# Query tiles from the last to the first inside each head of a differential-attention layer

## Chip, cores and metric

The kernel runs on 1 core of one Trainium2 chip. The metric is the device time of one execution in microseconds (us), the median of the runs shown.

## What is computed

One layer: differential attention with a causal mask, layer norm, a gated feed-forward network, layer norm. The part that the change touches is the attention core. With 2 batches of 2,048 tokens, 16 heads, head size 16 and values of size 32:

```python
s1 = jnp.einsum('bhqd,bhkd->bhqk', q1, k1) * scale
s2 = jnp.einsum('bhqd,bhkd->bhqk', q2, k2) * scale
a1 = jax.nn.softmax(jnp.where(causal, s1, neg_inf), axis=-1)
a2 = jax.nn.softmax(jnp.where(causal, s2, neg_inf), axis=-1)
comb = a1 - lam[None, :, None, None] * a2
out = jnp.einsum('bhqk,bhkv->bhqv', comb, v)
```

After it `out` is normalized per head, projected, added to `x` and normalized; then the feed-forward part follows.

## The kernel before

Five phases run one after the other, each with its own buffers: projections, a phase for the softmax shift, the attention (`attention_phase`), and the rest of the layer (`finish_phase`), which has a first form with rounded weights (the one that runs here) and a second one that is skipped. Only `attention_phase` is changed.

**Tiles and steps.** Inside a head the 2,048 queries are four query tiles t = 0, 1, 2, 3 of 512, and the keys are 16 blocks j of 128. A step (t, j) handles one key block against one query tile, for both batches and both softmaxes. Causality leaves tile t with 4t + 4 steps, 40 in a head. In the last four key blocks of a tile (the diagonal ones) the queries ahead of the key block are dropped, so a step is 512, 384, 256 or 128 queries wide; the four diagonal steps of a tile are a "512" with a mask, a "384", a "256" and a "128". The list `STEPS` writes the order out by hand. Named by width, with F for 512, it is:

- tile 0: F, 256, 128, 384
- tile 1: F, 256, F, 384, F, F, F, 128
- tile 2: F, F, 256, F, F, F, 384, F, F, F, F, 128
- tile 3: F, F, F, F, 256, F, F, F, F, 384, F, F, F, F, F, 128

**Units.** ScalarE does the exponentials. A step is two units, one per batch, except that a 256 or a 128 takes both batches in one. So a head has 72 units. Three score slots (`s_ps`, `SLOTS` = 3) hold one unit each, and four buffers (`probs`) one step each.

**TensorE's order.** For each step k TensorE issues the scores of k (L827), then the weighing with the values of step k - 3 (`LAG`, L847), and two steps after the weighing that ends a tile the transposes of its sums (`turn`, `TURN_LAG`, L855). So a tile's transposes stand behind the fifth step of what follows the tile:

```python
use(h, u, first, k - LAG)
if k - TURN_LAG in END:
    turn(h, END.index(k - TURN_LAG))
```

The scores of a unit wait until ScalarE has emptied its slot, three units earlier; the exponential (L808) waits for its scores; GpSimd masks the diagonal corner (L792); the weighing waits for exponential and mask.

**The sums.** Tile t adds up in PSUM bank t % 2. VectorE copies the finished bank out (L892), TensorE transposes it back into the bank, VectorE copies that out (L894), which frees the bank for the tile after the next, and six small operations (L902 to L913) finish the tile in `diff`. After the fourth tile of a head SyncE stores `diff` (L772) and then, once the head's weighing is over, loads the stacks of the head after the next (L517, L533, L540). Heads follow without a barrier: the scores of the next head are issued while the last three steps of this one are still to be weighed.

Of the kernel before, what the change touches and what calls it, by code (L numbers as in the profile page):

```python
# [29 lines left out]
QUERY_TILES = SEQ // TILE  # L30
# [658 lines left out]
def attention_phase(nc, keep, heads, qk_parts, shift, values, diffs):  # L689
# [2 lines left out]

    STEPS = [(0, j) for j in (0, 2, 3, 1)]
    for t in range(1, QUERY_TILES):
        third = SUBS * t // 3
        order = list(range(SUBS * t)) + [SUBS * t, SUBS * t + 3]
        order.insert(2 * third + SUBS * t % 3 // 2, SUBS * t + 1)
        order.insert(third, SUBS * t + 2)  # L700
        STEPS += [(t, j) for j in order]
    END = [max(k for k, (t, _) in enumerate(STEPS) if t == tile) for tile in range(QUERY_TILES)]

    UNITS = []
    for k, (t, j) in enumerate(STEPS):
        UNITS += [(k, [0, 1])] if j - SUBS * t >= SUBS // 2 else [(k, [0]), (k, [1])]
    NU = len(UNITS)
    LAST_UNIT = [max(n for n, (step, _) in enumerate(UNITS) if step == k) for k in range(len(STEPS))]
    LAG = 3
    TURN_LAG = 2  # L710

    MASKS = [sum(j >= SUBS * t for t, j in STEPS[:k + 1]) for k in range(len(STEPS))]
    NS = len(STEPS)
    NT = QUERY_TILES
    SLOTS = 3
    PROBS = 4
# [4 lines left out]
    def window(t, j):  # L721

        return max(0, j - SUBS * t) * PARTS

    with Room(nc, "attn") as room:
# [18 lines left out]
        probs_free = room.sem("probs_free")  # L744
        sums_copied = room.sem("sums_copied")
        turned = room.sem("turned")
        sums_bank_free = room.sem("sums_bank_free")
# [8 lines left out]
        def all_heads(head):  # L756

            for h in range(HEADS):
                head(h, h % 2, h // 2, h == 0, h == LAST)

        @block.sync
        def _(sp):
            def head(h, u, r, first, last):
                if not last:

                    sp.wait_ge(probs_free, PROBS + NS * h)
                    load_head(sp.dma_start, heads, qk_parts, values, h + 1, 1 - u)
                    load_shift(sp.dma_start, heads, shift, h + 1, 1 - u)

                sp.wait_ge(diff_ready, NT * h + NT)  # L770
                for b in range(BATCH):
                    sp.dma_start(diffs[b * KEY_BLOCKS:(b + 1) * KEY_BLOCKS, :, h, :].rearrange("k p n -> p k n"),  # L772
                                 diff[:, :, :].rearrange("p (k b) n -> p k b n", b=BATCH)[:, :, b, :]).then_inc(stored, 16)


            load_shift(sp.dma_start, heads, shift, 0, 0)
            all_heads(head)
            sp.wait_ge(stored, STORES + STORES * HEADS)
# [31 lines left out]
        @block.tensor  # L810
        def _(pe):
            def scores(h, u, r, first, n):

                k, batches = UNITS[n]
                t, j = STEPS[k]
                off = window(t, j)
                width = TILE - off
                if n == 0:

                    pe.wait_ge(loaded[u], 16 * HEAD_LOADS * r + 16 * HEAD_LOADS)  # L820
                if not first or n >= SLOTS:

                    pe.wait_ge(exp_done, NU * h + n - SLOTS + 1)
                for place, b in enumerate(batches):
                    for s in range(2):
                        rows = slice(s * HALF_ROWS, s * HALF_ROWS + STACK_ROWS)
                        last = nc.tensor.matmul(s_ps[n % SLOTS][:, s, place * width:(place + 1) * width],  # L827
                                                k_sb[u][rows, b * SEQ + j * PARTS:b * SEQ + (j + 1) * PARTS],
                                                q_sb[u][rows, b * SEQ + t * TILE + off:b * SEQ + (t + 1) * TILE], start=True, stop=True)
                last.then_inc(scored, 1)  # L830

            def weigh(h, u, k):

                t, j = STEPS[k]
                off = window(t, j)
                sums = sums_ps[t % 2]
                pe.wait_ge(exp_done, NU * h + LAST_UNIT[k] + 1)
                if j >= SUBS * t:

                    pe.wait_ge(masked, SUBS * NT * h + MASKS[k])  # L840
                if j == 0:

                    pe.wait_ge(sums_bank_free, NT * h + t + 1)
                for b in range(BATCH):
                    for s in range(2):
                        c = 2 * b + s
                        last = nc.tensor.matmul(sums[c * D:(c + 1) * D, off:TILE], v_sb[u][:, b * KEY_BLOCKS + j, :], probs[k % PROBS][:, b, s, off:TILE],  # L847
                                                start=(j == 0), stop=(k == END[t]))
                last.then_inc(probs_free, 1)

            def turn(h, t):

                pe.wait_ge(sums_copied, NT * h + t + 1)
                for i in range(SUBS):
                    last = nc.tensor.transpose(sums_ps[t % 2][:, i * PARTS:(i + 1) * PARTS], sums_sb[:, i * PARTS:(i + 1) * PARTS], keep["ident"][:, :])  # L855
                last.then_inc(turned, 1)

            def use(h, u, first, k):

                if k < 0:  # L860
                    if first:
                        return
                    h, u, k = h - 1, 1 - u, k + NS
                weigh(h, u, k)
                if k - TURN_LAG in END:
                    turn(h, END.index(k - TURN_LAG))
                elif k - TURN_LAG + NS in END and not first:
                    turn(h - 1, END.index(k - TURN_LAG + NS))

            def head(h, u, r, first, last):  # L870
                for k in range(NS):
                    for n, (step, _) in enumerate(UNITS):
                        if step == k:
                            scores(h, u, r, first, n)
                    use(h, u, first, k - LAG)
                if last:
                    for k in range(NS - LAG, NS):
                        use(h, u, first, k)
                    turn(h, QUERY_TILES - 1)

            all_heads(head)

        @block.vector
        def _(dve):
            def tile(h, t):
                n = NT * h + t
                bank = sums_ps[t % 2]


                dve.wait_ge(probs_free, PROBS + NS * h + END[t] + 1)  # L890
                dve.wait_ge(turned, n + 1)
                nc.vector.tensor_copy(sums_sb[:, :], bank[:, :]).then_inc(sums_copied, 1)  # L892
                dve.wait_ge(turned, n + 2)
                nc.vector.tensor_copy(raw[:, :, :, :].rearrange("p k s d -> p (k s d)"), bank[:, :]).then_inc(sums_bank_free, 1)  # L894


                v0 = VEC * n
                rows = diff[:, SUBS * BATCH * t:SUBS * BATCH * (t + 1), :]
                wide = [PARTS, SUBS * BATCH, D - 1]

                dve.wait_ge(sums_bank_free, 2 + n + 1)
                nc.vector.reciprocal(recip[:, :, :], raw[:, :, :, D - 1]).then_inc(vec, 1)  # L902
                dve.wait_ge(vec, v0 + 1)
                nc.vector.tensor_tensor(first[:, :, :], raw[:, :, 0, 0:D - 1], recip[:, :, 0:1].to_broadcast(wide), ALU.mult).then_inc(vec, 1)
                nc.vector.tensor_tensor(second[:, :, :], raw[:, :, 1, 0:D - 1], recip[:, :, 1:2].to_broadcast(wide), ALU.mult).then_inc(vec, 1)
                dve.wait_ge(vec, v0 + 3)

                dve.wait_ge(stored, STORES * h + STORES)
                nc.vector.scalar_tensor_tensor(rows[:, :, 0:D - 1], second[:, :, :], keep["neg_lam"][:, bass.ts(h, 1)], first[:, :, :], ALU.mult, ALU.add).then_inc(vec, 1)
                dve.wait_ge(vec, v0 + 4)  # L910
                nc.vector.tensor_reduce(total[:, :], rows[:, :, 0:D - 1], AXIS.X, ALU.add).then_inc(vec, 1)
                dve.wait_ge(vec, v0 + 5)
                nc.vector.tensor_scalar(rows[:, :, D - 1], total[:, :], -1.0, None, ALU.mult).then_inc(vec, 1)  # L913
                dve.wait_ge(vec, v0 + 6)
                dve.sem_inc(diff_ready, 1)

            for h in range(HEADS):
                for t in range(QUERY_TILES):
                    tile(h, t)


def turn_weights_phase(nc, keep, ffn_w, whole_w):
# [613 lines left out]
```

## Time and profile before

| | |
|---|---|
| median of 3 runs | 2055.02 us (2047.17 to 2059.04) |
| the profiled execution, its own time | 2058.76 us |
| its span, first to last instruction | 2057.0 us |
| attention phase, first scores to the issue of the last stores | 232.04 to 1279.42 us |
| one head in the middle of it | 64.61 us |
| TensorE (matmul) busy | 1917.9 us (93%) |
| ScalarE busy | 1468.7 us (71%) |
| VectorE busy | 724.0 us (35%) |

A row of a timeline gives the start in us, how long the piece lasts, engine, line, operation, the tiles, and how many instructions were joined in it; in brackets stands how long the engine had been idle before it and what released it. Pieces that follow one another with hardly a gap are joined. PE is TensorE, ACT ScalarE, DVE VectorE, SPq the queue of SyncE. The end of a matmul is modelled and overlaps the start of the next, so the cost of a piece on TensorE is the distance from its start to the next start.

### The profile page before, as it was taken

How to read it: one execution, taken by the hardware profiler on the slowest of the kernel's cores; microseconds unless marked ns; L12 is line 12 of the kernel's file. 1: busy time of each engine (PE TensorE's matmuls, PEld its weight loads, DVE VectorE, ACT ScalarE, POOL GpSimd, SP SyncE). 2: the span in 40 equal slices, each digit the busy share in tenths (PEclk: the TensorE clock that was granted, in tenths of full speed). 3: DMA queues.
4: the chain of work that ended last, by engine and by line, in shares of the span. 5: the costliest groups of instructions: out<-in, count | busy, mean ns of one | idle time of the engine just before them, and what ended most of it. 6: DMA issues, size and time to landing. Idle time of an engine off the chain costs nothing. (4 is left out here: it accounts for less than half of the span.)

```text
span 2057.0 us, 32689 instructions
## 1 busy us (share of the span) xinstructions
PE 1917.9 (93%) x12400; PEld 1091.7 (53%) x12400; DVE 724.0 (35%) x1543; ACT 1468.7 (71%) x1876; POOL 200.3 (10%) x300
## 2 busy tenths in 40 slices
PE   7995499999999999999999997599999999999996
PEld 6883133333333333333333332488888788888885
DVE  5776012222122221222112221445463545445342
ACT  5663499999999999999999997244454445445452
POOL 0001011111111111111111110000000000000000
PEclk9997699999999999999999999699999999999998
DMA  8997906643466434653356510200000000000000
GB/s 265 364 348 216 140 2 84 84 58 53 59 84 84 54 54 62 84 73 54 47 78 84 72 24 11 72 22 11 32 11 31 22 31 31 12 31 11 11 11 12
DMA packets 137048, 148.55 MB, mean 72 GB/s; under 512 B 76000, under 2 KB 108256, under 8 KB 133760
## 3 DMA queue, kind: packets, MB, share of 16 engines
q1 hardware_dynamic: 134768, 140.55, 34.2%
q10 hardware_dynamic: 1888, 5.24, 1.3%
q8 instruction: 104, 1.70, 0.4%
q0 software_dynamic: 240, 0.66, 0.2%
q14 instruction: 48, 0.39, 0.1%
HBM read 90.85 MB, written 55.57 MB: 71 GB/s over the span
## 5 line engine op out<-in xcount | busy, mean ns | idle before, releaser
L808 ACT ACTIVATE attn_probs<-attn_s_ps 128x1024 f32<-128x1024 f32 (+2 forms) x1152 | 1014.0, 1042 | 75.3 <-PE attn_s_ps L827 71.5
L847 PE MATMUL attn_sums_ps<-attn_probs,heads_v 128*32 128x512 f32 (+3 forms) x5120 | 603.1, 543 | 0.6 <-issue 0.6
L827 PE MATMUL attn_s_ps<-heads_q,heads_k 50*128 50x512 f32 (+3 forms) x2560 | 472.5, 431 | 67.2 <-DMA heads_q<-shift 49.5
L827 PEld LDWEIGHTS attn_s_ps<-heads_q,heads_k 50*128 50x128 f32 x2560 | 216.6, 185 | 543.1 <-ACT attn_probs L808 457.9
L1331 ACT ACTIVATE split_whole<-split_hid_ps,hs 128x512 f32<-128x512 f32 x128 | 88.3, 690 | 274.4 <-PE split_hid_ps L1245 274.2
L892 DVE COPY attn_sums_sb<-attn_sums_ps 128x512 f32<-128x512 f32 x64 | 44.3, 692 | 639.1 <-PE attn_sums_ps L847 635.7
L792 POOL TENSOR_SCALAR_AFFINE_SELECT attn_probs<-attn_probs 128x512 f32<-128x512 f32 x256 | 160.4, 635 | 919.8 <-ACT attn_probs L808 917.9
L1245 PE MATMUL split_hid_ps<-split_hid_b,h2t_r 128*128 128x512 f32 x1024 | 240.6, 392 | 0.0
L1245 PE MATMUL split_hid_ps<-split_hid_a,h1t_r 128*128 128x512 f32 x1024 | 238.0, 391 | 0.0
L1245 PEld LDWEIGHTS split_hid_ps<-split_hid_a,h1t_r 128*128 128x128 f32 x1024 | 190.0, 188 | 41.1 <-DVE split_hid_a L1473 1.3
L1245 PEld LDWEIGHTS split_hid_ps<-split_hid_b,h2t_r 128*128 128x128 f32 x1024 | 189.8, 188 | 38.0
L847 PEld LDWEIGHTS attn_sums_ps<-attn_probs,heads_v 128*32 128x32 f32 x5120 | 101.4, 108 | 165.3 <-issue 122.8
L1316 ACT ACTIVATE split_gate<-split_hid_ps,s 128x512 f32<-128x512 f32 x64 | 44.1, 689 | 94.4 <-PE split_hid_ps L1229 94.4
L894 DVE COPY attn_raw<-attn_sums_ps 128x512 f32<-128x512 f32 x64 | 44.2, 691 | 183.3 <-PE attn_sums_ps L855 183.3
L1479 DVE TENSOR_TENSOR split_hid_a<-split_whole,split_hid_a 128x512 fp32r<-128x512 f32 x64 | 44.3, 692 | 179.4 <-ACT split_hid_a L1334 179.4
L468 PE MATMUL proj_qk_ps<-proj_xt,proj_wqk_high 128*128 128x512 f32 x256 | 95.8, 420 | 1.5 <-DVE proj_xt L383 1.5
L1155 POOL TENSOR_TENSOR split_square<-split_heads 128x512 f32<-128x512 f32 x28 | 28.6, 1041 | 591.3 <-DVE split_head_var L1358 338.6
L1479 DVE TENSOR_TENSOR split_hid_b<-split_whole,split_hid_b 128x512 fp32r<-128x512 f32 x64 | 44.1, 689 | 94.8 <-ACT split_hid_b L1334 94.7
L1229 PE MATMUL split_hid_ps<-split_xt,w1t_r 128*128 128x512 f32 x256 | 72.2, 405 | 4.6 <-issue 3.2
L1229 PE MATMUL split_hid_ps<-split_xt,w2t_r 128*128 128x512 f32 x256 | 70.2, 397 | 0.0
L1469 DVE SCALAR_TENSOR_TENSOR split_whole<-split_hid_ps,s,split_gate 128x512 f32<-128x512 f32 x64 | 48.0, 751 | 54.3 <-ACT split_gate L1316 54.3
L1262 PE MATMUL split_y_ps<-w3t_r,split_hid_a 128*128 128x256 f32 x512 | 64.7, 284 | 2.6 <-DVE split_y L1503 2.6
(123 smaller groups left out, 1571.2 us busy)
## 6 DMA issues: line engine op xcount, KB each, us to landing
qk_parts<-proj_parts SPq DMA_DIRECT2D x64, 512.0 KB, 5.7
heads_q<-qk_parts SPq DMA_DIRECT2D x90, 256.0 KB
heads_k<-qk_parts SPq DMA_DIRECT2D x90, 256.0 KB
proj_w_rows<-in_L_ffn_h_w SPq DMA_DIRECT2D x16, 512.0 KB, 6.8
values<-proj_v SPq DMA_DIRECT2D x8, 1024.0 KB, 6.0
diffs<-attn_diff SPq DMA_DIRECT2D x32, 256.0 KB, 4.5
split_heads<-diffs SPq DMA_DIRECT2D x8, 1024.0 KB, 5.7
heads_v<-values SPq DMA_DIRECT2D x15, 512.0 KB
```

The source lines that it names most:

```text
L468: last = nc.tensor.matmul(qk_ps[m % 4][:, :], wqk[a][:, kind, c, o * PARTS:(o + 1) * PARTS], xt[u][b][:, c, :], start=(c == 0 and n == 0), ...
L792: pool.affine_select(out=corner, in_=corner, compare_op=ALU.is_ge, fill=0.0, base=0, pattern=[[0, 2 * BATCH], [1, PARTS]], channel_multipl ...
L808: nc.scalar.activation(weights, side_by_side, ACT.Exp, scale=SCALE).then_inc(exp_done, 1)
L827: last = nc.tensor.matmul(s_ps[n % SLOTS][:, s, place * width:(place + 1) * width], k_sb[u][rows, b * SEQ + j * PARTS:b * SEQ + (j + 1) * ...
L847: last = nc.tensor.matmul(sums[c * D:(c + 1) * D, off:TILE], v_sb[u][:, b * KEY_BLOCKS + j, :], probs[k % PROBS][:, b, s, off:TILE], start ...
L892: nc.vector.tensor_copy(sums_sb[:, :], bank[:, :]).then_inc(sums_copied, 1)
L1229: last = nc.tensor.matmul(bank[:, :], weights[w][:, c, m * PARTS:(m + 1) * PARTS], xt[k][:, c, :], start=(c == 0 and k == 0), stop=(c == E ...
L1245: last = nc.tensor.matmul(hid_ps[m % 4][:, :], weights[w][:, c, m * PARTS:(m + 1) * PARTS], hid[k][:, c, :], start=(c == 0 and k == 0), st ...
L1262: last = nc.tensor.matmul(y_ps[s % 2][:, s // 2, :], hid_a[k][:, c, s * PARTS:(s + 1) * PARTS], weights["w3t"][:, c, :], start=(c == 0 and ...
L1331: nc.scalar.activation(gelu, hid_ps[m % 4][:, :], ACT.Gelu, scale=keep[s][:, m:m + 1]).then_inc(gelu_done, 1)
L1469: nc.vector.scalar_tensor_tensor(product, hid_ps[2 * (m % 2) + 1][:, :], keep["s2"][:, m:m + 1], gate[m % 2][:, :], ALU.mult, ALU.mult).th ...
L1479: nc.vector.tensor_tensor(hid[1][:, m, :], whole[m % 2][:, :], hid[0][:, m, :].bitcast(F32), ALU.subtract).then_inc(hid_low, 1)
```

## The change

`STEPS` is built with the tiles in the order 3, 2, 1, 0. Inside a tile the order of the key blocks stays. The counters that ran with the tile's number now run with its place in the order.

```diff
-    STEPS = [(0, j) for j in (0, 2, 3, 1)]
-    for t in range(1, QUERY_TILES):
+    TILE_ORDER = list(reversed(range(QUERY_TILES)))
+    STEPS = []
+    for t in TILE_ORDER[:-1]:
...
         STEPS += [(t, j) for j in order]
-    END = [max(k for k, (t, _) in enumerate(STEPS) if t == tile) for tile in range(QUERY_TILES)]
+    STEPS += [(0, j) for j in (0, 2, 3, 1)]
+    END = [max(k for k, (t, _) in enumerate(STEPS) if t == tile) for tile in TILE_ORDER]
...
-                    pe.wait_ge(sums_bank_free, NT * h + t + 1)
+                    pe.wait_ge(sums_bank_free, NT * h + TILE_ORDER.index(t) + 1)
...
-                                                start=(j == 0), stop=(k == END[t]))
+                                                start=(j == 0), stop=(k in END))
...
-            def turn(h, t):
-
-                pe.wait_ge(sums_copied, NT * h + t + 1)
+            def turn(h, place):
+
+                t = TILE_ORDER[place]
+                pe.wait_ge(sums_copied, NT * h + place + 1)
...
-            def tile(h, t):
-                n = NT * h + t
+            def tile(h, place):
+                n = NT * h + place
+                t = TILE_ORDER[place]
...
-                dve.wait_ge(probs_free, PROBS + NS * h + END[t] + 1)
+                dve.wait_ge(probs_free, PROBS + NS * h + END[place] + 1)
...
-                for t in range(QUERY_TILES):
-                    tile(h, t)
+                for place in range(QUERY_TILES):
+                    tile(h, place)
```

What moves is shown at two places of TensorE's stream. `attn_s_ps` are the three score slots, `attn_sums_ps` the two banks of sums, `attn_sums_sb` is VectorE's copy of a finished bank; two score rows of 512 (or 384) columns are the two units of one step.

**First place, TensorE, where tile 1 begins.** Before, tile 1 follows tile 0 (its first three steps, a head other than the first):

```order
L827 MATMUL attn_s_ps0<-heads_q1,heads_k1 128x512 x2
L827 MATMUL attn_s_ps1<-heads_q1,heads_k1 128x512 x2
L847 MATMUL attn_sums_ps0<-attn_probs1,heads_v1 32x256 x4
L855 MATMUL attn_sums_ps1<-ident,attn_sums_sb 128x128 x4
L827 MATMUL attn_s_ps2<-heads_q1,heads_k1 128x256 x4
L847 MATMUL attn_sums_ps0<-attn_probs2,heads_v1 32x128 x4
L827 MATMUL attn_s_ps0<-heads_q1,heads_k1 128x512 x2
L827 MATMUL attn_s_ps1<-heads_q1,heads_k1 128x512 x2
L847 MATMUL attn_sums_ps0<-attn_probs3,heads_v1 32x384 x4
```

With the change it follows tile 2:

```order
L829 MATMUL attn_s_ps1<-heads_q0,heads_k0 128x512 x2
L829 MATMUL attn_s_ps2<-heads_q0,heads_k0 128x512 x2
L849 MATMUL attn_sums_ps0<-attn_probs1,heads_v0 32x512 x4
L829 MATMUL attn_s_ps0<-heads_q0,heads_k0 128x256 x4
L849 MATMUL attn_sums_ps0<-attn_probs2,heads_v0 32x512 x4
L829 MATMUL attn_s_ps1<-heads_q0,heads_k0 128x512 x2
L829 MATMUL attn_s_ps2<-heads_q0,heads_k0 128x512 x2
L849 MATMUL attn_sums_ps0<-attn_probs3,heads_v0 32x128 x4
```

The scores are the same (F, 256, F). Behind them stood the weighing of tile 0's narrow steps and the transposes of tile 3; now there stand two full steps and the 128 of tile 2.

**Second place, TensorE, the end of the phase.** Before, the last three weighings are tile 3's, and only its own transposes come after them:

```order
L827 MATMUL attn_s_ps2<-heads_q1,heads_k1 128x128 x4
L847 MATMUL attn_sums_ps1<-attn_probs0,heads_v1 32x512 x4
L847 MATMUL attn_sums_ps1<-attn_probs1,heads_v1 32x512 x4
L847 MATMUL attn_sums_ps1<-attn_probs2,heads_v1 32x512 x4
L847 MATMUL attn_sums_ps1<-attn_probs3,heads_v1 32x128 x4
L855 MATMUL attn_sums_ps1<-ident,attn_sums_sb 128x128 x4
```

With the change:

```order
L829 MATMUL attn_s_ps1<-heads_q1,heads_k1 128x384 x2
L829 MATMUL attn_s_ps2<-heads_q1,heads_k1 128x384 x2
L849 MATMUL attn_sums_ps0<-attn_probs0,heads_v1 32x512 x4
L849 MATMUL attn_sums_ps0<-attn_probs1,heads_v1 32x256 x4
L858 MATMUL attn_sums_ps1<-ident,attn_sums_sb 128x128 x4
L849 MATMUL attn_sums_ps0<-attn_probs2,heads_v1 32x128 x4
L849 MATMUL attn_sums_ps0<-attn_probs3,heads_v1 32x384 x4
L858 MATMUL attn_sums_ps0<-ident,attn_sums_sb 128x128 x4
```

The last tile is now tile 0, four narrow steps long, and the transposes of tile 1 stand between its weighings, two steps ahead of its own.

## Rows read from the trace of the kernel before

**Rows 1.** The page, part 5: the exponentials (busy, mean ns | idle before, releaser).

```profile
L808 ACT ACTIVATE attn_probs<-attn_s_ps 128x1024 f32<-128x1024 f32 (+2 forms) x1152 | 1014.0, 1042 | 75.3 <-PE attn_s_ps L827 71.5
```

**Rows 2.** Timeline of ScalarE, 560 to 640 us, one period of a head.

```profile
559.21 2.85 ACT L808 ACTIVATE attn_probs<-attn_s_ps 128x1024 f32<-128x1024 f32 x3 [0.21 <-PE attn_s_ps L827]
562.23 33.90 ACT L808 ACTIVATE attn_probs<-attn_s_ps 128x512 f32<-128x512 f32 x39 [0.16 <-PE attn_s_ps L827]
596.32 8.36 ACT L808 ACTIVATE attn_probs<-attn_s_ps 128x1024 f32<-128x1024 f32 x9 [0.20 <-PE attn_s_ps L827]
605.11 18.50 ACT L808 ACTIVATE attn_probs<-attn_s_ps 128x1024 f32<-128x1024 f32 x21 [0.43 <-PE attn_s_ps L827]
623.83 2.85 ACT L808 ACTIVATE attn_probs<-attn_s_ps 128x1024 f32<-128x1024 f32 x3 [0.21 <-PE attn_s_ps L827]
```

**Rows 3.** Groups by form, ScalarE, 304 to 1240 us: the full unit.

```profile
L808 ACT ACTIVATE attn_probs<-attn_s_ps 128x1024 f32<-128x1024 f32 x865 | 808.7, 1088 | 15.9 <-PE attn_s_ps L827 14.2
```

**Rows 4.** Timeline of TensorE, 558.5 to 566.5 us: from tile 3 into tile 0.

```profile
558.60 0.73 PE L827 MATMUL attn_s_ps<-heads_q,heads_k 50*128 50x512 f32 x4
...
560.26 0.50 PE L827 MATMUL attn_s_ps<-heads_q,heads_k 50*128 50x256 f32 x4
560.69 1.07 PE L847 MATMUL attn_sums_ps<-attn_probs,heads_v 128*32 128x512 f32 x8
561.69 0.44 PE L827 MATMUL attn_s_ps<-heads_q,heads_k 50*128 50x128 f32 x4
562.06 0.43 PE L847 MATMUL attn_sums_ps<-attn_probs,heads_v 128*32 128x128 f32 x8
562.41 0.64 PE L827 MATMUL attn_s_ps<-heads_q,heads_k 50*128 50x384 f32 x4
562.98 1.07 PE L847 MATMUL attn_sums_ps<-attn_probs,heads_v 128*32 128x512 f32 x8
563.98 0.73 PE L827 MATMUL attn_s_ps<-heads_q,heads_k 50*128 50x512 f32 x4
564.63 0.64 PE L847 MATMUL attn_sums_ps<-attn_probs,heads_v 128*32 128x256 f32 x8
565.21 0.66 PE L855 MATMUL attn_sums_ps<-ident,attn_sums_sb 128*128 128x128 f32 x4
565.79 0.50 PE L827 MATMUL attn_s_ps<-heads_q,heads_k 50*128 50x256 f32 x4
```

**Rows 5.** Timeline of ScalarE, 512.0 to 512.9 us: from tile 1 into tile 2.

```profile
511.31 1.77 ACT L808 ACTIVATE attn_probs<-attn_s_ps 128x512 f32<-128x512 f32 x2
```

**Rows 6.** Timeline of TensorE, 497 to 566 us.

```profile
502.63 0.85 PE L847 MATMUL attn_sums_ps<-attn_probs,heads_v 128*32 128x384 f32 x8
...
511.45 0.74 PE L827 MATMUL attn_s_ps<-heads_q,heads_k 50*128 50x512 f32 x4
...
536.45 0.50 PE L827 MATMUL attn_s_ps<-heads_q,heads_k 50*128 50x512 f32 x2 [0.41 <-ACT attn_probs L808]
...
539.89 0.73 PE L827 MATMUL attn_s_ps<-heads_q,heads_k 50*128 50x512 f32 x4
```

**Rows 7.** Timeline of VectorE, 497 to 566 us: tile 3, then tile 0.

```profile
501.29 0.69 DVE L894 COPY attn_raw<-attn_sums_ps 128x512 f32<-128x512 f32 x1 [2.66 <-PE attn_sums_ps L855]
...
504.76 0.69 DVE L892 COPY attn_sums_sb<-attn_sums_ps 128x512 f32<-128x512 f32 x1 [0.23 <-DVE attn_diff L913]
```

**Rows 8.** Timeline of all engines, 1240 to 1300 us: the end of the phase.

```profile
1271.42 0.44 PE L827 MATMUL attn_s_ps<-heads_q,heads_k 50*128 50x128 f32 x4
...
1274.98 0.69 DVE L892 COPY attn_sums_sb<-attn_sums_ps 128x512 f32<-128x512 f32 x1 [17.87 <-PE attn_sums_ps L847]
...
1279.42 1.44 SPq L772 DMA_DIRECT2D diffs<-attn_diff  x2
```

**Rows 9.** Windows: busy us of PE, PEld, DVE, ACT, POOL, then PEclk, DMA share, GB/s.

```profile
232.00:246.70 14.70, 13.87 (x72) 5.22 (x72) 0.69 (x1) 11.16 (x13) 3.13 (x5) 0.52 1.03 125
536.00:558.60 22.60, 21.77 (x160) 6.82 (x158) 3.02 (x8) 22.17 (x26) 1.27 (x2) 1.00 0.00 1
```

## The prediction

> **What bounds the kernel now.** Only the attention phase changes, so I read it alone. The page's groups come first: the exponentials on ScalarE are busy 1014.0 us of a phase of some 1047, and 71.5 of the 75.3 us that ScalarE idled ahead of them were ended by scores [rows 1]. So inside the phase ScalarE is the bound, and what the order can change is the time it waits for scores. The timeline of ScalarE shows where that is: a head repeats after 623.83 - 559.21 = 64.62 us, with four visible gaps [rows 2].
>
> To price the gaps I need the cost of one unit. Nine full units last 8.36 us [rows 2], one alone 1.09 [rows 3], so the next starts every (8.36 - 1.09) / 8 = 0.91 us. A 384 unit (768 elements of 1024) is then about 0.68, a 128 unit (512) 0.45. A head has 60 full-sized units, 8 of 384 and 4 of 128: 54.5 + 5.4 + 1.8 = 61.6 us. **ScalarE loses 3.0 us in each head**, and these 3.0 us are the whole subject.
>
> Where they go, each as the next start less the start before plus its work [rows 2]:
> - tile 3 into tile 0, first F after the 128: 21 units from 605.11 are 18.1 us of work, free at 623.2, next at 623.83: 0.60.
> - the 128 of tile 0: free at 559.21 + 2.72 = 561.93, starts at 562.23: 0.30.
> - the two next steps of tile 0. TensorE's rows give the time from the start of a score piece to the start of its exponential: 0.61 for an F (558.60 to 559.21), 0.54 for a 128 (561.69 to 562.23) [rows 2, 4]. The 384 at 562.41 and the F at 563.98 so start 0.28 and 0.26 late.
> - tile 1 into tile 2: the 128 starts at 511.31, is free at 511.76, the F issued at 511.45 starts at 512.06: 0.30 [rows 5, 6].
> - tile 2 into tile 3: 0.64 ahead of 605.11 [rows 2], behind the transposes of tile 2; and about 0.5 ahead of 596.32, from what is left of 39 units. The rest, 0.15, lies at the transposes inside tile 2.
>
> Each loss is a place where TensorE, which does a full step in 0.66 + 1.00 = 1.66 us against ScalarE's 1.81, has had extra work or a narrow unit has shortened the backlog. In long runs of F it catches up and waits for a slot (0.41 at 536.45 [rows 6]); then the backlog is three units again.
>
> **The change, part by part.** Nothing is added or removed: the same 40 steps, 72 units, 4 transposes and 4 VectorE chains per head. Only the junctions between tiles differ: 3|0, 0|1, 1|2, 2|3 become 3|2, 2|1, 1|0, 0|3. TensorE's prices, start to start [rows 4]: scores F 0.66, 384 0.57, 256 0.43, 128 0.36; weighing F 1.00, 256 0.58, 128 0.35; transposes 0.58. The weighing of a 384 is 0.85 less the modelled 0.07, 0.78 [rows 6].
>
> - **3|2**: the tail of tile 3 costs what it did, 0.60; the head of tile 2 behind a gap is as it was, 0.15. Sum 0.75 (before these were 0.60 and 0.15 too, elsewhere).
> - **2|1**: the tail of tile 2 costs 0.5. Then F, 256, F is issued behind full weighings instead of tile 0's narrow ones. From the start of tile 1: the second F is issued at 1.66 + 0.43 + 1.00 = 3.09 and can start at 3.70; ScalarE started at 0.61 and is free after three units at 3.34. New loss 0.36. Behind it stands the weighing of only 128 (0.35), and TensorE pulls ahead. At the transposes of tile 2, behind the fifth step, I walk on the same way: the next F can start at 8.5, ScalarE is free at 8.7, no loss. Sum 0.86.
> - **1|0**: going on with the walk, tile 0's first F can start at 12.9 and ScalarE is free at 12.7: 0.2 in place of 0.60. Then the 128, the 384 as before: 0.30 + 0.28. Sum 0.78.
> - **0|3**: the F after the 384 0.26 as before. The transposes of tile 1 stand behind it as those of tile 3 did. Then come weighings of 128 and 384, TensorE runs ahead until it waits for a slot, as it did at 536.45, and from there to the F behind the transposes (539.89 [rows 6]) the instructions are word for word those of before: 0.64. Sum 0.90.
>
> After: 0.75 + 0.86 + 0.78 + 0.90 = 3.29 against 3.0: **+0.27 us per head**, over 16 heads +4.3. As the errors of such a walk are about 0.1 at each of four junctions, its bounds are -0.1 and +0.6 per head: -2 to +10.
>
> **The end of the phase.** Before, the last unit (the 128 of tile 3) was issued at 1271.42, the last copy began at 1274.98, the stores went out at 1279.42 [rows 8]; its exponential starts 0.92 after the issue and is 0.45 of work, so 6.6 us pass from ScalarE's last work to the stores. After, the last scores are tile 0's 384. Behind them come weighing F, weighing 256 and the transposes of tile 1 at 0.57 + 1.00 + 0.58 = 2.15. VectorE copies the result 0.70 later (the transposes at 565.21 [rows 4] stood a period earlier at 500.59, the copy at 501.29 [rows 7]) and needs 504.76 - 501.29 = 3.47 us for the chain of that tile before it takes the next copy [rows 7]; TensorE's own last weighing would have been over sooner. The last copy so starts at 6.3, the stores 4.44 later at 10.7. ScalarE's work ended at 1.9. 8.8 against 6.6: **+2.2 us**. Inside the phase the same queue on VectorE costs nothing, because tile 0's transposes are four steps later.
>
> **The start.** In head 0 the granted clock is 0.52 of full for 14.7 us while TensorE is busy 13.87 of them [rows 9], the lower level of 1.2 GHz. There TensorE is the bound in either order, and 13.87 us at half speed are the same work. Tile 3 first puts more exponentials per matmul into this stretch, tile 0 first fewer; I take 0, bounds -2 and +2.
>
> **What costs nothing.** The bank wait: tile 3's first weighing waits for the bank of tile 1, freed by a copy behind the transposes, four steps earlier, as now between 3 and 1. The stores and the loads of the head after the next leave SyncE later by about 1.3 us (tile 0's transposes are behind the fifth step of a wide tile, not a narrow one), and the loads are over long ahead of the next head: DMA share 0.00 in the last 22.6 us [rows 9]. Without that cover each us late would be a us for the head.
>
> **Sum**: +4.3 + 2.2 + 0 = +6.5 us. On the profiled execution's own 2058.76 that is 2065.3. The median of the runs is 3.74 lower, so the forecast as a median is **2061.5 us**, its own range 2053 to 2069 (bounds of the walk, of the start, and some 4 us between runs).
>
> **Rivals.**
> - **Slower, the transposes starve tile 1.** At tile 1's fifth step my walk leaves 0.2 us of backlog. If it is under 0, the transposes cost ScalarE there what they cost in tile 3, up to 0.64. For it: tile 1 has the fewest F in a row ahead of them. Against: the weighing of 128 just before. Decides once TensorE is 0.2 us later than I have it. +10 over 16 heads: 2072.
> - **Faster, tile 0 behind a backlog.** If tile 1's run of F leaves a full backlog, the losses of tile 0 (0.2 + 0.30 + 0.28 + 0.26) and tile 1's 0.36 vanish: -22, so 2040. Against: at 1|2 the same tail left 0.30 of loss [rows 5].
> - **No change.** The junction losses only move, and the end costs its 2.2: 2057. The narrow tile stands between two others in both orders.
> - **The clock.** TensorE is idle for 0.8 us of the 14.7 and the clock stays at its lower level. If wide steps make it rise a third of the way in, some 10 us run at 2.4 instead of 1.2 GHz: -5, so 2056.5. The Trainium skill, page "TensorE: Matmul & The Clock Gate", Part 1, says that the throttled clock is the default and that sustained activity releases it; by that rule the denser start should be released sooner, and the time would be this rival's. The trace of before speaks against it, with 13.87 busy us at the lower level [rows 9], so it gets little.
>
> **How the numbers follow.** Forecast 0.65, no change 0.13, the clock 0.05, slower 0.12, faster 0.05. A measurement of this kernel can tell about 0.5%, 10.3 us, from no change. Faster by more: the faster rival, 0.05. Slower by more: the slower rival and the upper edge of the forecast, 0.17. Same: 0.78. The range takes the no-change case and the lower half of the slower one: 2050 to 2071.
>
> **What would show it.** In the profile after, a head should repeat after 64.9 us. ScalarE should show gaps at the start of tile 2, of tile 1 and again 2.7 us later, a smaller one at tile 0's start, and one of 0.43 behind the transposes in tile 3. At the end the last L892 copy should be released by L913, not by a weighing. I am wrong if the period is under 64.5 or over 65.3, if ScalarE has a gap behind tile 1's fifth step, or if TensorE ever waits for L892 or L894 inside the phase.

## The result, and the profile after

| | before | after |
|---|---|---|
| median of 20 runs | 2055.09 us | 2059.76 us |
| lowest to highest | 2047.17 to 2059.04 | 2055.38 to 2065.88 |
| ratio, 95% interval | | 1.0027, 1.0017 to 1.0037 |
| profiled execution, span | 2057.0 us | 2055.6 us |
| first scores to the issue of the last stores | 1047.4 us | 1049.3 us |
| one head in the middle | 64.62 us | 64.95 us |

The change makes the kernel 4.7 us (0.2%) slower, clear of noise, and less than the 0.5% that the prediction counted as no change. The two profiled executions stand the other way round, 2058.76 us before and 2057.33 after (spans 2057.0 and 2055.6). By the traces the attention phase itself is 1.9 us longer after the change; the phases ahead of it took 2.1 us less (it begins at 229.93 in place of 232.04) and the rest of the layer 1.2 us less, though neither was changed. What else parts the two is told below.

The page after (busy us, share and count of TensorE; then the groups that answer to [rows 1] and the copies of finished banks):

```profile
PE 1917.7 (93%) x12400; PEld 1089.8 (53%) x12400; DVE 719.2 (35%) x1543; ACT 1470.8 (72%) x1876; POOL 200.9 (10%) x300
...
L810 ACT ACTIVATE attn_probs<-attn_s_ps 128x1024 f32<-128x1024 f32 (+2 forms) x1152 | 1015.8, 1033 | 71.7 <-PE attn_s_ps L829 67.9
...
L896 DVE COPY attn_sums_sb<-attn_sums_ps 128x512 f32<-128x512 f32 x64 | 44.3, 692 | 654.7 <-PE attn_sums_ps L849 651.1
```

Idle time ahead of the exponentials did not grow in this page, 71.7 us for 75.3 before, since the wait ahead of the phase (47.3 us, before 49.1), the first head and two stalled heads of the kernel before are in it. In every other head it rose, from 1.3 to 1.4 or 1.5 us. The page cannot show that; the timeline can. ScalarE from 560 to 700 us, one period of a head, answering to [rows 2] (start, length, joined instructions, idle time ahead):

```profile
565.49 18.51 ACT L810 ACTIVATE attn_probs<-attn_s_ps 128x1024 f32<-128x1024 f32 x21 [0.43 <-PE attn_s_ps L829]
584.20 19.45 ACT L810 ACTIVATE attn_probs<-attn_s_ps 128x1024 f32<-128x1024 f32 x22 [0.21 <-PE attn_s_ps L829]
603.85 2.86 ACT L810 ACTIVATE attn_probs<-attn_s_ps 128x1024 f32<-128x1024 f32 x3 [0.20 <-PE attn_s_ps L829]
606.93 12.22 ACT L810 ACTIVATE attn_probs<-attn_s_ps 128x1024 f32<-128x1024 f32 x14 [0.23 <-PE attn_s_ps L829]
619.33 10.68 ACT L810 ACTIVATE attn_probs<-attn_s_ps 128x512 f32<-128x512 f32 x12 [0.18 <-PE attn_s_ps L829]
630.43 18.50 ACT L810 ACTIVATE attn_probs<-attn_s_ps 128x1024 f32<-128x1024 f32 x21 [0.43 <-PE attn_s_ps L829]
```

Two of these rows are joined across a tile's end. From 565.49 to 630.43 a head repeats after 64.94 us, and there are five visible gaps where [rows 2] has four. The new one is 0.23 ahead of 606.93, three units behind the start of tile 1 (603.85). With the unit costs of the prediction the losses are: 0.6 at 584.20 (tile 3 into 2), 0.6 from there to 603.85 (inside tile 2, and 2 into 1), 0.37 at 606.93, 0.6 up to 619.33 (tile 1 into 0 and the 128), 1.1 up to 630.43 (the rest of tile 0, 0 into 3, the transposes): 3.3 us. A loss is larger than the idle time in brackets, because the records of neighbouring exponentials overlap; where a row runs on, a loss can hide in it.

TensorE at the same place, the start of tile 1, with the F behind the 256, the slot wait and the transposes:

```profile
603.25 0.73 PE L829 MATMUL attn_s_ps<-heads_q,heads_k 50*128 50x512 f32 x4
...
606.33 0.73 PE L829 MATMUL attn_s_ps<-heads_q,heads_k 50*128 50x512 f32 x4
...
608.01 0.44 PE L829 MATMUL attn_s_ps<-heads_q,heads_k 50*128 50x384 f32 x2 [0.22 <-ACT attn_probs L810]
...
610.63 0.66 PE L858 MATMUL attn_sums_ps<-ident,attn_sums_sb 128*128 128x128 f32 x4
```

The F behind the 256 is issued 606.33 - 603.25 = 3.08 us behind the start of the tile. One and a half steps later TensorE already waits 0.22 us for a slot, so at the transposes (610.63) ScalarE has a backlog and shows no gap.

The end of the phase (TensorE's last scores, the transposes of tile 1, the last copy, the stores), answering to [rows 8]:

```profile
1268.79 2.24 ACT L810 ACTIVATE attn_probs<-attn_s_ps 128x512 f32<-128x512 f32 x3 [0.18 <-PE attn_s_ps L829]
...
1268.97 0.61 PE L829 MATMUL attn_s_ps<-heads_q,heads_k 50*128 50x384 f32 x4
...
1270.94 0.66 PE L858 MATMUL attn_sums_ps<-ident,attn_sums_sb 128*128 128x128 f32 x4
...
1271.64 0.69 DVE L898 COPY attn_raw<-attn_sums_ps 128x512 f32<-128x512 f32 x1 [1.83 <-PE attn_sums_ps L858]
...
1274.79 0.69 DVE L896 COPY attn_sums_sb<-attn_sums_ps 128x512 f32<-128x512 f32 x1 [0.23 <-DVE attn_diff L917]
...
1275.54 0.66 PE L858 MATMUL attn_sums_ps<-ident,attn_sums_sb 128*128 128x128 f32 x4 [2.71 <-DVE attn_sums_sb L896]
...
1279.24 1.45 SPq L774 DMA_DIRECT2D diffs<-attn_diff  x2
```

The last copy is released by L917, the end of tile 1's chain on VectorE, and TensorE stands 2.71 us until it is there (0.81 before). From the last scores to the stores it takes 10.27 us, before 8.00. ScalarE's last work ends at 1271.03, so 8.2 us pass from there to the stores; before they were 6.2 (ScalarE's last row ended at 1273.18, the stores went out at 1279.42): +2.0 us. Counted as the prediction counts it, from the start of the last exponential plus its cost, it is 8.3 against 6.6, +1.7 us.

### The profile page after: what moved, and what is told of

Read it like the earlier page. It is cut to its first block and busy times, and to the rows that moved or that the text cites. A ratio compares the mean times of both kernels' runs of the same rounds, so it can differ in the third digit from the quotient of the medians.

```text
span 2055.6 us, 32689 instructions
## 1 busy us (share of the span) xinstructions
PE 1917.7 (93%) x12400; PEld 1089.8 (53%) x12400; DVE 719.2 (35%) x1543; ACT 1470.8 (72%) x1876; POOL 200.9 (10%) x300
## 5 line engine op out<-in xcount | busy, mean ns | idle before, releaser
L810 ACT ACTIVATE attn_probs<-attn_s_ps 128x1024 f32<-128x1024 f32 (+2 forms) x1152 | 1015.8, 1033 | 71.7 <-PE attn_s_ps L829 67.9
L829 PE MATMUL attn_s_ps<-heads_q,heads_k 50*128 50x512 f32 (+3 forms) x2560 | 476.6, 432 | 64.9 <-DMA heads_q<-shift 47.7
## 6 DMA issues: line engine op xcount, KB each, us to landing
qk_parts<-proj_parts SPq DMA_DIRECT2D x64, 512.0 KB, 5.8
proj_w_rows<-in_L_ffn_h_w SPq DMA_DIRECT2D x16, 512.0 KB, 6.6
heads_v<-values SPq DMA_DIRECT2D x15, 512.0 KB
```

What stands on the lines that cost most here:

```text
L810: nc.scalar.activation(weights, side_by_side, ACT.Exp, scale=SCALE).then_inc(exp_done, 1)
```

## The experiments

All expectations were on record before the run. Every kernel of this section has its steps written out in a table `BLOCKS_OF`, one list of key blocks for each tile, in place of the loop that built them, so its line numbers lie one below those of the change; where nothing else is said the lists are those of before. The kernel before ran again beside each group, and ratios are against those runs. The time of a head is read as the distance between rows of ScalarE or VectorE one head apart. Apart from the first head and from single stalled ones (last section) it repeats within 0.02 us, with steps of 0.1 us in `e1_fwd_last0`, so one profile tells it better than the medians: the single runs of one kernel spread over 10 us.

### Where the order turns, and what stands last

`e1_fwd_last0` keeps the junctions of before and puts tile 0 last:

```diff
-    TILE_ORDER = list(reversed(range(QUERY_TILES)))
+    TILE_ORDER = [1, 2, 3, 0]
```

> Tiles in the order 1, 2, 3, 0: the same junctions inside the loop as before (0|1, 1|2, 2|3, 3|0), but tile 0 is the last tile of the phase. Junction theory: a head repeats after 64.62 us as before, and only the end of the phase grows, 10.3 us from the last scores to the issue of the last stores in place of 8.0 (about +2 us on the median, apart from the start). Rival (what counts is which tile opens and closes a head, since the loads and the stores of a head stand there): 64.95 us as after the change.

ScalarE, one period (681.39 is the F behind tile 3, 684.41 the 128 of tile 0, 718.52 the start of tile 3):

```profile
681.39 2.85 ACT L809 ACTIVATE attn_probs<-attn_s_ps 128x1024 f32<-128x1024 f32 x3 [0.21 <-PE attn_s_ps L828]
684.41 33.90 ACT L809 ACTIVATE attn_probs<-attn_s_ps 128x512 f32<-128x512 f32 x39 [0.16 <-PE attn_s_ps L828]
718.52 8.36 ACT L809 ACTIVATE attn_probs<-attn_s_ps 128x1024 f32<-128x1024 f32 x9 [0.21 <-PE attn_s_ps L828]
```

```profile
1266.37 0.64 PE L828 MATMUL attn_s_ps<-heads_q,heads_k 50*128 50x384 f32 x4
...
1272.21 0.69 DVE L895 COPY attn_sums_sb<-attn_sums_ps 128x512 f32<-128x512 f32 x1 [0.23 <-DVE attn_diff L916]
...
1276.91 1.45 SPq L773 DMA_DIRECT2D diffs<-attn_diff  x2
```

From one head to the next it takes 64.62 us, and 64.72 four times in fifteen. The second piece, all engines at the end, has the last scores, last copy and stores: 10.54 us, the copy again behind L916, the end of the chain of the tile ahead. Median 2056.73 us against 2054.55, ratio 1.0007 (0.9994 to 1.0020). So by the traces the end costs some 2 us more when tile 0 is last, with the junctions of before here and with the new ones after the change, and the heads hardly care which tile opens them. The medians are 2.2 us apart, within an interval that holds nothing as well.

`e2_rev_last3` has the junctions of the change and tile 3 last:

```diff
-    TILE_ORDER = list(reversed(range(QUERY_TILES)))
+    TILE_ORDER = [2, 1, 0, 3]
```

> Tiles in the order 2, 1, 0, 3: the junctions of the change (3|2, 2|1, 1|0, 0|3), but tile 3 is the last of the phase. Junction theory: 64.95 us per head, 8.0 us from the last scores to the stores, median some 5 us over before. Rival (opening and closing tile): 64.62 us.

```profile
603.41 18.51 ACT L809 ACTIVATE attn_probs<-attn_s_ps 128x1024 f32<-128x1024 f32 x21 [0.43 <-PE attn_s_ps L828]
...
668.36 18.50 ACT L809 ACTIVATE attn_probs<-attn_s_ps 128x1024 f32<-128x1024 f32 x21 [0.43 <-PE attn_s_ps L828]
```

64.95 us per head (668.36 - 603.41) and 8.00 us at the end (last scores 1271.38, stores 1279.38), both as expected. The median was 2063.59 us, ratio 1.0054 (1.0034 to 1.0073): 9 us over before where 5 were expected. A miss of 4 us, taken up below.

### Which junction it is

Two orders need the bank of sums chosen by place, since neighbours now can have the same parity:

```diff
-    TILE_ORDER = list(reversed(range(QUERY_TILES)))
+    TILE_ORDER = [0, 1, 3, 2]
...
-                sums = sums_ps[t % 2]
+                sums = sums_ps[TILE_ORDER.index(t) % 2]
```

(and `place % 2` in the transposes and on VectorE.) `e9_keep_23` is the same with `[2, 3, 1, 0]`.

> Tiles in the order 0, 1, 3, 2, with the bank of sums taken by place instead of by tile (both parities of neighbours become possible). Only the junction 0|1 of before is kept; 1|3, 3|2 and 2|0 are new. If the 0.33 us come from tile 1 no longer standing behind tile 0, whose narrow weighings let TensorE feed ScalarE in time: 64.62 us per head as before. Rival (each junction has its own price, so any reordering moves the sum; or the descending direction costs): between 64.7 and 65.0 us.

> Tiles in the order 2, 3, 1, 0, bank by place. It keeps 2|3 of before and takes 1|0 and 3|1; tile 1 stands behind tile 3. Theory (tile 1 must stand behind tile 0): 64.95 us per head, the whole loss of the change although half of the order ascends, with a gap at the F behind the 256 of tile 1. Rival (direction, or each junction its own price): some value between 64.6 and 64.9 us.

ScalarE in `e8_keep_01`, 0, 1, 3, 2; four gaps per head, 711.46 - 646.85 = 64.61 us:

```profile
646.85 18.50 ACT L809 ACTIVATE attn_probs<-attn_s_ps 128x1024 f32<-128x1024 f32 x21 [0.42 <-PE attn_s_ps L828]
...
685.22 2.85 ACT L809 ACTIVATE attn_probs<-attn_s_ps 128x1024 f32<-128x1024 f32 x3 [0.20 <-PE attn_s_ps L828]
688.24 22.79 ACT L809 ACTIVATE attn_probs<-attn_s_ps 128x512 f32<-128x512 f32 x26 [0.17 <-PE attn_s_ps L828]
711.46 18.50 ACT L809 ACTIVATE attn_probs<-attn_s_ps 128x1024 f32<-128x1024 f32 x21 [0.43 <-PE attn_s_ps L828]
```

ScalarE in `e9_keep_23`, 2, 3, 1, 0; 676.12 - 611.20 = 64.92 us, with the gap of 0.22 three units behind the start of tile 1 (611.20):

```profile
611.20 2.85 ACT L809 ACTIVATE attn_probs<-attn_s_ps 128x1024 f32<-128x1024 f32 x3 [0.21 <-PE attn_s_ps L828]
614.28 12.21 ACT L809 ACTIVATE attn_probs<-attn_s_ps 128x1024 f32<-128x1024 f32 x14 [0.22 <-PE attn_s_ps L828]
626.66 21.77 ACT L809 ACTIVATE attn_probs<-attn_s_ps 128x512 f32<-128x512 f32 x25 [0.17 <-PE attn_s_ps L828]
...
676.12 2.85 ACT L809 ACTIVATE attn_probs<-attn_s_ps 128x1024 f32<-128x1024 f32 x3 [0.21 <-PE attn_s_ps L828]
```

Medians 2054.18 us (0.9984, 0.9969 to 0.9999) and 2060.49 us (1.0027, 1.0016 to 1.0039). One junction decides. With tile 1 behind tile 0 a head takes 64.6 us although three of the four junctions are other ones than before; with tile 1 behind tile 3 it takes 64.9, half of the order ascending.

The slower orders also share a second new junction, tile 0 behind tile 1, so the times of a head alone do not tell the two apart. The places of the losses do. In the traces of before, the change, `e1_fwd_last0`, `e2_rev_last3`, `e8_keep_01` and `e9_keep_23`, take from the distance between neighbouring starts on ScalarE the cost of the unit (0.90 us for a full one, medians over heads 3 to 14). The loss ahead of a tile then goes by the tile that ended, whichever comes next: 0.6 us behind tile 3, 0.5 behind tile 2, 0.3 behind tile 1, 0.2 behind tile 0. Behind tile 1 it is 0.30 when tile 2 follows, 0.29 when tile 3 does and 0.27 when tile 0 does. One loss alone comes and goes with the neighbour: at the F behind the 256 of tile 1, 0.36 behind tile 2, 0.35 behind tile 3, and none behind tile 0. That is the 0.33 us, but for the 0.03 that is saved behind tile 1, and direction as such costs nothing.

### The losses are local and can be moved

In both kernels the largest single loss, 0.64 us, stands in tile 3, where the transposes of the tile ahead come behind the 256-wide step. `e4_fwd_t3late` and `e7_rev_t3late` move that step, in the order of before and of the change:

```diff
-        3: [0, 1, 2, 3, 14, 4, 5, 6, 7, 13, 8, 9, 10, 11, 12, 15],
+        3: [0, 1, 2, 3, 4, 5, 6, 7, 14, 8, 9, 10, 13, 11, 12, 15],
```

> Tiles 0, 1, 2, 3 as before, but in tile 3 the 256-wide step moves from the fifth to the ninth place and the 384 to the thirteenth (F x8, 256, F F F, 384, F F, 128). In both kernels the transposes of the tile ahead stand behind that 256, and ScalarE loses 0.64 us there. Junction theory: that loss shrinks to some 0.1, a head repeats after 63.9 us in place of 64.62, the kernel is about 11 us faster (0.5%). Rival (the time of a head is TensorE's or VectorE's work, the gaps are slack that returns elsewhere): 64.6 us.

> The same move inside tile 3, with the tiles in the order 3, 2, 1, 0. Junction theory: the losses are local and add up, so the head repeats after 64.25 us, still 0.33 above its forward twin. Rival (the gaps compete for one slack): the difference between the two orders changes.

ScalarE in `e4_fwd_t3late` and in `e7_rev_t3late`:

```profile
619.94 33.88 ACT L809 ACTIVATE attn_probs<-attn_s_ps 128x512 f32<-128x512 f32 x39 [0.17 <-PE attn_s_ps L828]
654.02 29.64 ACT L809 ACTIVATE attn_probs<-attn_s_ps 128x1024 f32<-128x1024 f32 x33 [0.20 <-PE attn_s_ps L828]
683.83 33.88 ACT L809 ACTIVATE attn_probs<-attn_s_ps 128x512 f32<-128x512 f32 x39 [0.17 <-PE attn_s_ps L828]
```

```profile
605.10 12.22 ACT L809 ACTIVATE attn_probs<-attn_s_ps 128x1024 f32<-128x1024 f32 x14 [0.23 <-PE attn_s_ps L828]
617.49 48.57 ACT L809 ACTIVATE attn_probs<-attn_s_ps 128x512 f32<-128x512 f32 x55 [0.18 <-PE attn_s_ps L828]
666.27 2.86 ACT L809 ACTIVATE attn_probs<-attn_s_ps 128x1024 f32<-128x1024 f32 x3 [0.21 <-PE attn_s_ps L828]
669.35 12.21 ACT L809 ACTIVATE attn_probs<-attn_s_ps 128x1024 f32<-128x1024 f32 x14 [0.22 <-PE attn_s_ps L828]
```

The gap of 0.43 is gone from both. 683.83 - 619.94 = 63.89 us and 669.35 - 605.10 = 64.25 us: 0.7 less each, and the difference between the two orders, 0.36, stayed. By the distances between starts the 256 at its new place lost about what was expected (0.62 us became 0.14 and 0.12), but that is 0.5 of the 0.7 us: the rest came from the end of tile 3, where the later 384 stands now and where the loss fell from 0.6 to 0.3. The expectation had not named this. Medians 2043.11 us against 2055.90 (0.9933, 0.9912 to 0.9954) and 2049.62 (0.9968, 0.9956 to 0.9979).

### Placing all narrow steps

`e5_fwd_spread` and `e6_rev_spread` write out all four lists (here the first; the second has the tiles 3 to 0 and its own lists):

```diff
+        0: [0, 3, 2, 1],
+        1: [0, 6, 1, 5, 4, 2, 3, 7],
+        2: [0, 9, 1, 2, 3, 4, 5, 10, 8, 6, 7, 11],
+        3: [0, 1, 2, 3, 4, 5, 6, 13, 12, 7, 14, 8, 9, 15, 10, 11],
```

> Tiles 0, 1, 2, 3, all diagonal steps placed anew: each narrow score step stands so that it is issued about three steps behind another narrow step, whose narrow weighing then follows it, and no transposes stand behind a narrow step (tile 0: F 128 384... as 512, 128, 256, 384; the others with their 512 diagonal step apart from the last step). By walking on with the costs of single pieces: 63.2 us per head, 1.4 less than before, about 22 us on the kernel (1.1%). Rival: 64.6, or a new wait on masks (GpSimd) that eats it.

> Tiles 3, 2, 1, 0 with diagonal steps placed by the same walk for this order. Theory: 63.2 us per head as well, so that the direction costs nothing once the narrow steps are placed for it; only the end (+2 us) stays. Rival (descending order costs by itself): 0.3 us above its forward twin.

ScalarE in `e5_fwd_spread`, the whole of two heads without a gap that would part the row:

```profile
599.55 136.32 ACT L809 ACTIVATE attn_probs<-attn_s_ps 128x1024 f32<-128x1024 f32 x155
```

63.17 us per head, 63.2 expected; median 2032.37 us against 2055.90, ratio 0.9886 (0.9868 to 0.9905). No wait for the masks shows on TensorE. The losses are not all gone, they fell from 3.1 to 1.7 us per head by the distances between starts. This profile has two stalled heads, 1.1 and 1.8 us longer. `e6_rev_spread` takes 63.26 us per head, median 2034.86 us (0.9898, 0.988 to 0.9916). The direction that cost 0.33 us per head costs 0.1 once the narrow steps are placed for it. What was changed at once in these lists was not tested piece by piece. Both beat the kernel before and the change; the forward one, 1.1% faster, is the version to take.

## Why the prediction was right

- **The bound and the size of the loss.** ScalarE's 3.0 us of loss per head was the right thing to read. The sum had a slip, 54.5 + 5.4 + 1.8 is 61.7 and not 61.6, and a full unit starts every 0.90 us in the traces where I had 0.91; with that the losses are 3.1 before and 3.5 after, and their difference is the same. The walk gave 3.29 after the change; 3.3 was measured with its own unit costs. Per head +0.33 us where +0.27 was forecast, in bounds of -0.1 to +0.6; over 15 distances between heads that is 5.0 us.
- **Junction by junction.** Ahead of tile 2 0.60 forecast, 0.6 measured; inside tile 2 and ahead of tile 1 0.15 + 0.5 forecast, 0.6 measured. The new loss at the F behind the 256 0.36, measured 0.37, with its issue forecast at 3.09 us and found at 3.08. No loss at tile 1's transposes was forecast, and none was found. 1|0 with the 128 0.5, measured 0.6: the loss ahead of tile 0 is 0.27 by the distance between starts, where the walk had 0.2, and it is the term that made 0.27 out of 0.33 per head. It parts no row, so the smaller gap forecast at tile 0's start cannot be seen in the timeline as it is printed. 0|3 with the rest of tile 0 1.18, measured 1.1.
- **The end.** +2.2 us forecast, +2.0 measured from ScalarE's last work, by the cause that was named: the copy released by the chain of tile 1. From the last scores I had 10.7 us, and it was 10.27; tile 1's transposes start 1.97 us behind the scores, not 2.15, and VectorE's chain from one copy to the next takes 1274.79 - 1271.64 = 3.15 us, not 3.47.
- **The start.** Taken as 0 with bounds of 2 us. In the profiled pair it was not 0: the first head is 3.2 us longer than the later ones before and 1.1 after, so this pair gains 2.1 us there. The windows of the two profiles (busy us of PE, PEld, DVE, ACT, POOL, then the granted clock), after and then before; the first scores stand at 229.93 and 232.04:

```profile
229.00:239.50 10.50, 8.76 (x32) 3.17 (x36) 0.00 (x0) 7.88 (x9) 0.00 (x0) 0.50 0.96 134
239.50:242.00 2.50, 2.50 (x22) 0.64 (x16) 0.00 (x0) 1.82 (x3) 0.65 (x1) 1.00 1.15 164
```

```profile
232.00:246.20 14.20, 13.37 (x72) 5.22 (x72) 0.69 (x1) 10.67 (x13) 3.13 (x5) 0.50 0.98 119
246.20:248.00 1.80, 1.80 (x21) 0.52 (x14) 0.00 (x0) 1.19 (x2) 0.63 (x1) 1.00 0.98 118
```

The lower level, 1.2 GHz, ended 9.6 us behind the first scores after the change and 14.1 us before it; in the profiles of the experiments it ended after 7.5 to 11.8 us, without regard to the order (8.7, 7.5 and 11.5 with tile 0 first as before, 11.2 and 11.8 with tile 3 first as after). Half of the 4.5 us, 2.3, is about what the first head of the profiled execution after gained. The kernel before also had two heads of 66.2 and 66.3 us in its profile, 3.4 us more than undisturbed heads, with the one behind them. Without these the profile after would be the longer one, as the medians are. The clock rival names an effect of the right size, but it moves by as much between profiles that begin with the same tile, so nothing shows that the wide steps cause it, and what the order does to the start of the medians stays open.
- **The sum.** +6.5 us forecast, +4.7 measured by the medians, interval +3.5 to +7.6. The number is less well founded than the mechanism: the heads and the end come to 7.0 by the traces; that the medians show 2.3 less lies within the interval and within what the start and the stalls below move, and was not taken apart further.

The slower rival fell with the missing gap at tile 1's fifth step, the faster one with the losses in tile 0, the no-change case, in which the end alone stays, with the interval: its +2.2 us lie below +3.5.

## What to carry to other kernels

Where two engines are nearly balanced behind a short buffer, the order of steps is not free: price each junction of unlike steps by walking both engines through it, with start-to-start costs from one profile. Nothing extra (the transposes) should stand behind a narrow step; moving the 256 away from them was tried with one list. The other rule, a narrow score step where a narrow weighing follows it, was followed in the two spread lists together with the first and was not tried alone. Before reversing a loop to gain something else, look at which pair of neighbours it parts; here only 0|1 mattered.

## What was not expected

**Stalls of TensorE without a releaser.** The miss of `e2_rev_last3` led to two more looks at the same kernel:

> The order 2, 1, 0, 3 once more, for its median of 2063.6 us, 4 us above what 64.95 us per head give. Its first profile has three heads of 65.46 us, in which ScalarE's gap behind the 384 step of tile 0 is 0.61 us. If its slower executions are those in which more heads fall into that pattern, a profile over 2060 us has more than three of them and each costs 0.51 us; if they come from elsewhere (the clock at the start), the heads are 64.95 us and the clock is lower.

> The same kernel a third time, to see whether the number of 65.46 us heads follows the time.

They took 2063.0 and 2059.25 us, a single run of the kernel before beside them 2061.24, and neither theory held. Counted from head to head, 65.46 us occurs once in fifteen in the first profile, never in the second, once in the third (I had read distances from every tile, which show one late piece up to four times). But each profile has longer heads at about the same place, the tenth to twelfth distance: +1.2 us in the first, +4.7 in the second, +2.2 and +0.9 in the third. TensorE in the second look:

```profile
854.66 0.50 PE L828 MATMUL attn_s_ps<-heads_q,heads_k 50*128 50x512 f32 x2
858.54 0.51 PE L828 MATMUL attn_s_ps<-heads_q,heads_k 50*128 50x512 f32 x2 [3.38 <-issue]
...
862.63 0.73 PE L828 MATMUL attn_s_ps<-heads_q,heads_k 50*128 50x512 f32 x4
```

It waits 3.38 us between two halves of one step, and the cause is given as "issue": the profile shows nothing that it waited for. The clock follows (busy us of five engines, then the granted clock):

```profile
845.00:853.00 8.00, 8.00 (x72) 2.68 (x72) 2.69 (x7) 7.82 (x10) 1.93 (x4) 1.00 1.10 127
...
857.00:860.00 3.00, 1.46 (x11) 0.50 (x12) 0.00 (x0) 0.92 (x1) 0.00 (x0) 0.86 0.71 78
860.00:863.00 3.00, 3.00 (x20) 1.58 (x20) 1.90 (x5) 1.31 (x3) 0.00 (x0) 0.57 0.59 162
```

Behind the 3.4 us of standing the level is at its lower value for part of 857 to 863 us, and the head takes 4.7 us more in all. The kernel before has such heads too (66.17 and 66.28, behind each other), and so has `e5_fwd_spread` (64.30 and 64.95 for 63.17); the change, `e6_rev_spread`, `e7_rev_t3late`, `e8_keep_01` and `e9_keep_23` have none over 0.05 us. This one lies where the next head's loads run (DMA share 1.10 in the first window). The traces have eight such stalls of TensorE, 0.6 to 3.4 us long, and each ends 1.5 to 1.8 us behind the landing of a packet of 16 KB of the queue q8, kind "instruction", that took 1.7 to 2.0 us; most such packets take 0.9 to 1.4. That points to a late fetch of instructions. It does not show it: every profile has 12 to 16 of 16 KB that took over 1.5 us in the phase, those without a stall too, and no run tested it. It would be 1 to 5 us of a kernel's spread, and a candidate for the 4 us by which `e2_rev_last3` missed, which stays open; of its order the profiles show 64.95 us per head and nothing more.

**The length of the slow clock at the start** varies from 7.5 to 14.1 us between profiles with much the same work in it, which is worth up to 3.3 us by an estimate, half of the difference. The first head was 0.9 to 3.2 us longer than the later ones. The Trainium skill, page "TensorE: Matmul & The Clock Gate", Part 1, calls the transition run-variable. The profiles here agree: three of the one kernel with the order 2, 1, 0, 3 have 9.5, 10.8 and 8.4 us.
